# Filling an attention and feed-forward pipeline on one core: activation table loaded in advance, VectorE splits the first batch, the second batch's projections moved, dummy products on TensorE

## The chip, the cores and the metric

The kernel runs on one core of a Trainium2 chip. The metric is the device time of one execution in microseconds (us), lower is better. The engines are TensorE (PE in the profile; PEld is its weight load), VectorE (DVE), ScalarE (ACT), GpSimd (POOL) and SyncE (SP), whose queue issues all of the kernel's DMAs.

## What is computed

32 batches of 256 tokens by 128 channels. Each is layer-normalised; the normalised batch goes through 16-head attention (head size 8) and through a gated feed-forward part with token shift; both are added to the input.

```python
xn = _layernorm(x, axis=-1)
x = x + attn(xn, wq, bq, wk, bk, wv, bv, wo, bo) + ffn(xn, W_r, W_k, W_v, mu_r, mu_k)

# attn
q, k, v = (einsum('bsd,hde->bhse', x, w) + b for each of the three)
scores = softmax(einsum('bhse,bhte->bhst', q, k) * scale, axis=-1)
att = einsum('bhst,bhte->bhse', scores, v)
return att.transpose(0, 2, 1, 3).reshape(b, s, h * e) @ wo.T + bo

# ffn
xr, xk = mu * x + (1 - mu) * x_prev          # mu_r and mu_k
return sigmoid(xr @ W_r.T) * (square(relu(xk @ W_k.T)) @ W_v.T)
```

## The kernel before

The work is a software pipeline written out by hand, one step for each batch. `steps` calls each engine's `step(t, ...)` for t from -4 to 32; t = 4 to 27 stand in a hardware loop, the rest is straight code. In step t the engines work on several batches at once: t + 4 (statistics of the layer norm), t + 3 (normalise, transpose, project to q and k), t + 2 (split q and k into parts), t + 1 (row maxima of the scores), t (exponentials and their product with the values), t - 1 (output projection, store). `live(d)` says whether batch t + d exists, so the steps before t = 0 hold only the stages that already have a batch. `n(d)` is the count that a semaphore has reached when batch t + d is done.

A batch goes through these stages, by the names in the code:

- VectorE: `bn_stats`, `bn_aggr`, `var_eps`; GpSimd: `rstd` (a power), then `xn` (L316, two instructions).
- TensorE transposes `xn` (L616), ScalarE copies the result to `xn_t` (L412).
- TensorE projects `xn_t` to q in bank `misc_c` (L658) and k in `misc_b` (L662). ScalarE rounds each to bfloat16, `qk_h` (L380); VectorE subtracts, `qk_rest` (L454); GpSimd rounds the rest, `qk_m` (L328), and subtracts again, `qk_l` (L330). Three bfloat16 parts of q and k thus stand for float32.
- SyncE writes the parts to a DRAM tensor `spill` (L236 for h and m, L229 for l) and reads them back in the layout of the score products, `ops`, in two halves of two DMAs each (L214). The read waits for all five writes of the batch.
- For each of the 16 heads u, TensorE makes the scores a first time (L572, `bank_max`, two products), from 48 rows of `ops` in one half of the array's rows; VectorE reduces them to a maximum (L473). One step later it makes them a second time with the negated maxima as three added rows (L567, `bank_exp`), and ScalarE takes the exponential (L398). `LEAD` = 2: the maxima run two heads ahead, so the maxima of heads 0 and 1 of the next batch fall in u = 14 and 15 of a step. From t = 0 on, each exponential's product stands beside a maximum's product of the other half of the rows. In t = -1 the maxima of the first batch stand alone.
- In step t = -1 the first exponentials don't exist yet; TensorE ends it at u = 15 with the projections of batch 2 and the hidden product of batch 0 (L668), and t = 0 begins.

Other lines that matter: all of ScalarE's work waits for the weights' three DMAs (L368), and so does all of GpSimd's step work (L284). ScalarE's table load is put by the build ahead of its first activation. In t = -3, u = 11, VectorE fills constants (`fill_constants`, L441 to L448), ahead of the first `qk_rest`.

Of the kernel before, what the change touches and what calls it, by code (L numbers as in the profile page):

```python
# [7 lines left out]
ALU = mybir.AluOpType  # L8
# [40 lines left out]


# [5 lines left out]
def split_attention_ffn_kernel(nc, x, weights, columns, bo, out):  # L56
# [4 lines left out]
    with ExitStack() as ctx:  # L61
# [6 lines left out]
        def sem(name):  # L68
            return ctx.enter_context(nc.semaphore(name))
# [12 lines left out]
        rstd = sb("rstd", [P, ST])  # L82
        xn = sb("xn", [P, ST, D])
# [46 lines left out]
                                                         sem("rstd_done"))  # L130
        xn_done, xn_t_psum, xn_t_done = sem("xn_done"), sem("xn_t_psum"), sem("xn_t_done")
# [146 lines left out]
        def _(pool):  # L278
# [5 lines left out]
            pool.wait_ge(weights_in, 16 * N_WEIGHT_DMAS)  # L284
# [19 lines left out]
            def step(t, c, n, moved, paired, quad, live):  # L304
                p = c % 2
                if live(3):
                    pool.wait_ge(rstd_done, n(3))
                    after(pool, xn_t_psum, n(2))
                if live(2):
                    after(pool, rest_done, n(-2))  # L310
                    nc.gpsimd.tensor_tensor(x_bo[(c + 2) % TURN][:, :, :], x_in[(c + 2) % TURN][:, :, :],  # L311
                                            bo_all[:, :].unsqueeze(1).broadcast_to([P, ST, D]),
                                            ALU.add).then_inc(x_bo_done, 1)
                if live(3):
                    for i in range(ST):
                        last = nc.gpsimd.tensor_scalar(xn[:, i, :], x_in[(c + 3) % TURN][:, i, :], moments[:, i, 0:1],  # L316
                                                       rstd[:, i:i + 1], ALU.subtract, ALU.mult)
                    last.then_inc(xn_done, 1)
# [8 lines left out]
                if live(2):  # L327
                    nc.gpsimd.tensor_copy(qk_m[:, :, :], qk_rest[:, :, :]).then_inc(m_done, 1)  # L328
                    pool.wait_ge(m_done, n(2))
                    nc.gpsimd.tensor_tensor(qk_l[:, :, :], qk_rest[:, :, :], qk_m[:, :, :],  # L330
                                            ALU.subtract).then_inc(l_done, 1)
# [35 lines left out]
        def _(act):  # L367
            act.wait_ge(weights_in, 16 * N_WEIGHT_DMAS)  # L368
# [62 lines left out]
        def _(dve):  # L431
# [25 lines left out]

            by_head = misc_b[:, :].rearrange("p (k w) -> p k w", w=VW)

            def step(t, c, n, moved, paired, quad, live):  # L460
                p = c % 2
                for u in range(H):
# [12 lines left out]
                    if u == 1 and live(2):  # L475
                        take_high(1, misc_b, n(2), n(1))
                    if u == 5 and live(-1):
                        dve.wait_ge(tokens_psum, n(-1))
                        nc.vector.reciprocal(inv_den[:, :], by_head[:, :, E]).then_inc(inv_done, 1)
                        dve.wait_ge(inv_done, n(-1))  # L480
                        after(dve, att_t_psum, n(-2))
                        nc.vector.tensor_tensor(att[:, :, :], by_head[:, :, 0:E],
                                                inv_den[:, :].unsqueeze(2).broadcast_to([P, ST * H, E]),
                                                ALU.mult).then_inc(att_done, 1)
# [12 lines left out]
                    if u == 11 and live(4):  # L497
                        for i in range(ST):
# [5 lines left out]
                                                ALU.add).then_inc(var_done, 1)  # L504
                    if u == 11 and live(3) and not live(2):
                        dve.wait_ge(weights_in, 16 * N_WEIGHT_DMAS)
                        dve.wait_ge(ident_made, 1)
                        fill_constants()
# [13 lines left out]
        def _(pe):  # L522
            pe.wait_ge(ident_made, 1)

# [22 lines left out]

            def step(t, c, n, moved, paired, quad, live):
                p = c % 2
                for u in range(H):  # L550
# [3 lines left out]
                    if live(0):  # L554

                        if u % HALF == 0:
                            pe.wait_ge(shift_in[hf], moved(0, 2))
                        after(pe, exp_done[(u - 2) % H], n(0) if u >= 2 else n(-1))
                    if live(ahead):
# [4 lines left out]
                    for i in range(ST):  # L564
                        if live(0):
                            rows = slice(RG * r, RG * r + KE)
                            exp_mm = nc.tensor.matmul(bank_exp[r][:, i, :], ops[p][rows, hf, 1, pr, i * P:(i + 1) * P],  # L567
                                                      ops[p][rows, hf, 0, pr, :], start=True, stop=True)
                        if live(ahead):
# [81 lines left out]
                    if u == 15 and live(3):  # L651
                        moving = xn_t[(c + 3) % TURN][:, 1:1 + S]
                        pe.wait_ge(xn_t_done, n(3))
                        after(pe, shift_done[0], n(1))
                        after(pe, qk_rest_done[0], n(2))
                        if not live(2):
                            pe.wait_ge(weights_in, 16 * N_WEIGHT_DMAS)
                        nc.tensor.matmul(misc_c[:, 0:S], w[:, W_Q, :], moving, start=True,  # L658
                                         stop=True).then_inc(qk_psum[0], 1)
                        after(pe, val_done, n(1))  # L660
                        after(pe, qk_rest_done[1], n(2))
                        nc.tensor.matmul(misc_b[:, 0:S], w[:, W_K, :], moving, start=True,  # L662
                                         stop=True).then_inc(qk_psum[1], 1)
# [43 lines left out]
```

## Time and profile before

| | |
|---|---|
| median of 3 runs | 494.83 us (493.98 to 497.01) |
| the profiled execution's own time | 495.58 us |
| its span | 493.8 us |
| busy: PE, DVE, ACT, POOL | 457.5, 420.4, 385.2, 341.7 us |
| chain that ended last, share of PE | 85% |

The span is what the profiler sees between the first and the last instruction. The filling reaches to the first exponential product, at 39.75 us; the rest is 32 steps and the end of the pipeline. Busy TensorE time is modelled from pipelined products, so a share of 93% does not mean that the array is at its peak.

### The profile page before, as it was taken

The numbers are of one execution on the slowest core, as the hardware profiler recorded it, in microseconds if no ns is written. First come the engines' busy times: TensorE is split into PE (matmuls) and PEld (weight loads), VectorE is DVE, ScalarE is ACT, GpSimd is POOL, SyncE is SP. The second block draws the span as 40 slices with busy tenths as digits, with TensorE's granted clock in tenths as the row PEclk, the third lists the DMA queues.
The fourth block names the chain that finished last, engine by engine and source line by source line (L and its number), as shares of the span: only waits on it lengthen the run. The fifth ranks groups of instructions, "written<-read, shape, count | busy, mean of one in ns | idle before, by whom it ended". The sixth has DMA issues, their size and how long they took to land.

```text
span 493.8 us, 15503 instructions
## 1 busy us (share of the span) xinstructions
PE 457.5 (93%) x5184; PEld 260.3 (53%) x5184; DVE 420.4 (85%) x882; ACT 385.2 (78%) x833; POOL 341.7 (69%) x615
## 2 busy tenths in 40 slices
PE   1379999999999999999999999999999999999994
PEld 1125555555555555555555565556555555555552
DVE  4287899999998999899998999999998999988831
ACT  1117888887888888888888888888888888888883
POOL 6657777777787777777777777777877777776220
PEclk9999999999999999999999999999999999999997
DMA  2443454354554544345544543445544444455100
GB/s 85 127 128 81 139 153 126 95 145 130 149 152 120 151 125 118 108 134 150 150 143 126 135 127 109 124 140 150 149 124 133 131 120 119 130 141 141 46 16 22
DMA packets 85837, 60.43 MB, mean 122 GB/s; under 512 B 6192, under 2 KB 73392, under 8 KB 85808
## 3 DMA queue, kind: packets, MB, share of 16 engines
q1 hardware_dynamic: 85808, 60.06, 43.0%
q8 instruction: 16, 0.26, 0.2%
q14 instruction: 13, 0.11, 0.1%
HBM read 29.89 MB, written 29.36 MB: 120 GB/s over the span
## 4 chain that ended last, share of the span: by engine, by line
PE 85%; DVE 5%; issue 4%; ACT 2%; DMA 2%; POOL 1%; DVEq 0%; ACTq 0%; SPq 0%; POOLq 0%
PE bank_exp L567 24%; PE bank_val L535 24%; PE bank_max L572 6%; PE misc_b L638 4%; PE misc_a L589 4%; PE misc_a L608 4%; PE misc_c L658 4%; DVE neg_max L473 4%; PE misc_a L646 3%; PE misc_b L599 3%; PE misc_b L662 3%; PE misc_a L668 2%; PE misc_b L621 1%; PE misc_c L616 1%; PE misc_c L543 1%
## 5 line engine op out<-in xcount | busy, mean ns | idle before, releaser
L473 DVE TENSOR_REDUCE neg_max<-bank_max 128x2 f32<-128x512 f32 x512 | 329.5, 686 | 38.5 <-PE bank_max L572 33.4
L398 ACT ACTIVATE probs<-bank_exp 128x512 f32<-128x512 f32 x512 | 278.9, 598 | 47.2 <-PE bank_exp L567 44.8
L572 PE MATMUL bank_max<-ops 48*128 48x256 bf16 x1024 | 174.6, 278 | 10.7 <-DMA ops<-spill 8.2
L567 PE MATMUL bank_exp<-ops 51*128 51x256 bf16 x1024 | 169.5, 271 | 8.7 <-DVE neg_max L473 2.7
L535 PE MATMUL bank_val<-probs,val 128*25 128x256 f32 x2048 | 138.4, 383 | 1.2 <-ACT probs L398 1.2
L567 PEld LDWEIGHTS bank_exp<-ops 51*128 51x128 bf16 x1024 | 65.7, 94 | 110.0 <-issue 89.0
L535 PEld LDWEIGHTS bank_val<-probs,val 128*25 128x25 f32 x2048 | 56.5, 103 | 41.1 <-issue 20.2
L572 PEld LDWEIGHTS bank_max<-ops 48*128 48x128 bf16 x1024 | 61.2, 94 | 17.6 <-DMA ops<-spill 8.6
L316 POOL TENSOR_SCALAR xn<-x_in,moments,rstd 128x128 f32<-128x128 f32 x64 | 50.6, 798 | 0.1
L360 POOL TENSOR_TENSOR rstd<-var_eps,minus_half 128x2 f32<-128x2 f32 x32 | 22.8, 714 | 38.6 <-DVE var_eps L503 36.0
L355 POOL TENSOR_TENSOR mixed_x<-mixed_x,xn_t 128x512 f32<-128x512 f32 x32 | 40.6, 1270 | 2.5
L326 POOL TENSOR_TENSOR act_sq<-act_r 128x256 f32<-128x256 f32 x32 | 19.6, 612 | 28.7 <-issue 19.2
L330 POOL TENSOR_TENSOR qk_l<-qk_rest,qk_m 128x512 bf16<-128x512 f32 x32 | 37.2, 1162 | 2.6
L294 POOL TENSOR_TENSOR max_parts<-neg_max,zeros 128x16 bf16<-128x16 f32 x64 | 13.9, 218 | 31.9 <-DVE neg_max L473 31.9
L351 POOL TENSOR_TENSOR mixed_x<-dx,col 128x512 f32<-128x512 f32 x32 | 33.4, 1042 | 2.5
L373 ACT COPY shift<-misc_c 24x256 bf16<-24x256 bf16 x64 | 22.7, 355 | 14.0 <-PE misc_c L543 14.0
L380 ACT ACTIVATE qk_h<-misc_c,col 128x256 bf16<-128x256 f32 x32 | 15.2, 476 | 14.8 <-PE misc_c L658 14.2
L336 POOL TENSOR_TENSOR rest<-ffn,x_bo 128x256 f32<-128x256 f32 x32 | 23.1, 722 | 4.5 <-DVE ffn L494 4.5
L311 POOL TENSOR_TENSOR x_bo<-x_in,bo_all 128x256 f32<-128x256 f32 x32 | 23.5, 735 | 3.6 <-issue 3.4
L658 PE MATMUL misc_c<-xn_t,w 128*128 128x256 f32 x64 | 23.9, 458 | 1.8 <-ACT xn_t L412 1.8
L328 POOL CAST qk_m<-qk_rest 128x512 bf16<-128x512 f32 x32 | 19.5, 609 | 7.2 <-issue 5.1
L638 PE MATMUL misc_b<-w,xn_t 128*128 128x128 f32 x128 | 23.3, 306 | 0.0
(59 smaller groups left out, 591.7 us busy)
## 6 DMA issues: line engine op xcount, KB each, us to landing
ops<-spill SPq DMA_DIRECT2D x128, 192.0 KB, 3.4
spill<-qk_h SPq DMA_DIRECT2D x64, 192.0 KB, 3.3
spill<-qk_m SPq DMA_DIRECT2D x64, 128.0 KB, 1.9
x_in<-x SPq DMA_DIRECT2D x32, 128.0 KB, 2.1
spill<-qk_l SPq DMA_DIRECT2D x32, 128.0 KB, 1.8
y_out<-y SPq DMA_DIRECT2D x32, 128.0 KB, 1.9
ops<-shift SPq DMA_DIRECT2D x128, 6.0 KB
w<-weights SPq DMA_DIRECT2D x1, 448.0 KB, 3.1
```

The source lines that it names most:

```text
L311: nc.gpsimd.tensor_tensor(x_bo[(c + 2) % TURN][:, :, :], x_in[(c + 2) % TURN][:, :, :], bo_all[:, :].unsqueeze(1).broadcast_to([P, ST, D]) ...
L316: last = nc.gpsimd.tensor_scalar(xn[:, i, :], x_in[(c + 3) % TURN][:, i, :], moments[:, i, 0:1], rstd[:, i:i + 1], ALU.subtract, ALU.mult)
L330: nc.gpsimd.tensor_tensor(qk_l[:, :, :], qk_rest[:, :, :], qk_m[:, :, :], ALU.subtract).then_inc(l_done, 1)
L351: nc.gpsimd.tensor_tensor(mix[:, :, :], dx[:, :].unsqueeze(1).broadcast_to([P, 2, S]), col[:, C_MUR:C_MUK + 1].unsqueeze(2).broadcast_to([ ...
L355: nc.gpsimd.tensor_tensor(mix[:, :, :], mix[:, :, :], prev.unsqueeze(1).broadcast_to([P, 2, S]), ALU.add).then_inc(mix_tokens_done, 1)
L398: nc.scalar.activation(probs[g % 2][:, u % G, :, :], bank_exp[u % 2][:, :, :], ACT.Exp, scale=SCALE).then_inc(exp_done[u], 1)
L473: nc.vector.tensor_reduce(out=neg_max[hf][:, :, r, pr], in_=bank_max[v % 2][:, :, :], axis=AX_X, op=ALU.max, negate=True).then_inc(max_don ...
L535: last = nc.tensor.matmul(bank_val[SW * j:SW * j + MW, g // 2, :], weights[:, 0:MW] if fresh else weights[:, VW:VW + MW], probs[g % 2][:, ...
L567: exp_mm = nc.tensor.matmul(bank_exp[r][:, i, :], ops[p][rows, hf, 1, pr, i * P:(i + 1) * P], ops[p][rows, hf, 0, pr, :], start=True, stop ...
L572: max_mm = nc.tensor.matmul(bank_max[r][:, i, :], of[rows, max_hf, 0, max_pr, i * P:(i + 1) * P], of[rows, max_hf, 1, max_pr, :], start=Tr ...
L638: last = nc.tensor.matmul(misc_b[:, i * D:(i + 1) * D], xn_t[(c + 1) % TURN][:, 1 + i * P:1 + (i + 1) * P], w[:, W_V, :], start=True, stop ...
L658: nc.tensor.matmul(misc_c[:, 0:S], w[:, W_Q, :], moving, start=True, stop=True).then_inc(qk_psum[0], 1)
```

## The change

Six edits, all in the steps before t = 0:

- ScalarE waits for the constants alone and does one tiny `Exp` into `scratch` before it waits for the weights.
- GpSimd no longer waits for the weights before its first `rstd`; it waits for them ahead of its first `x_bo`, in t = -2.
- The first batch's `xn` is made by VectorE, `normalise_first`, right behind the first `var_eps`.
- The first batch's `qk_m` and `qk_l` are made by VectorE, `split_first`, right behind its second `qk_rest`.
- The q and k projections, now a function `project`, stand for batch 1 at u = 8 of t = -2, ahead of the first maxima; before, they stood at u = 15, behind the first two heads' maxima. All other batches keep u = 15.
- TensorE does nine 128x128 float32 products of the identity with itself (`WARM`) into `misc_a` before anything else, and, in each head whose maximum has no exponential beside it (16 heads of t = -1, two of t = -2), a dummy product into `bank_exp` beside each of the two products of the maximum, from the other half of the rows.

```diff
+WARM = 9
@@ gpsimd
-            pool.wait_ge(weights_in, 16 * N_WEIGHT_DMAS)
             pool.wait_ge(consts_made, 1)
...
-                if live(3):
+                if live(3) and live(2):
                     pool.wait_ge(rstd_done, n(3))
                     after(pool, xn_t_psum, n(2))
                 if live(2):
+                    if not live(1):
+                        pool.wait_ge(weights_in, 16 * N_WEIGHT_DMAS)
...
-                if live(3):
+                if live(3) and live(2):
                     for i in range(ST):
                         last = nc.gpsimd.tensor_scalar(xn[:, i, :], x_in[(c + 3) % TURN][:, i, :], moments[:, i, 0:1],
...
-                if live(2):
+                if live(2) and live(1):
                     nc.gpsimd.tensor_copy(qk_m[:, :, :], qk_rest[:, :, :]).then_inc(m_done, 1)
@@ scalar
+            act.wait_ge(consts_made, 1)
+            nc.scalar.activation(scratch[:, :], minus_half[:, :], ACT.Exp).then_inc(tables_in, 1)
             act.wait_ge(weights_in, 16 * N_WEIGHT_DMAS)
@@ vector
+            def normalise_first():
+                dve.wait_ge(rstd_done, 1)
+                for i in range(ST):
+                    last = nc.vector.tensor_scalar(xn[:, i, :], x_in[0][:, i, :], moments[:, i, 0:1],
+                                                   rstd[:, i:i + 1], ALU.subtract, ALU.mult)
+                last.then_inc(xn_done, 1)
+
+            def split_first():
+                dve.wait_ge(qk_rest_done[0], 1)
+                dve.wait_ge(qk_rest_done[1], 1)
+                nc.vector.tensor_copy(qk_m[:, :, :], qk_rest[:, :, :]).then_inc(m_done, 1)
+                dve.wait_ge(m_done, 1)
+                nc.vector.tensor_tensor(qk_l[:, :, :], qk_rest[:, :, :], qk_m[:, :, :], ALU.subtract).then_inc(l_done, 1)
...
                     if u == 1 and live(2):
                         take_high(1, misc_b, n(2), n(1))
+                        if not live(1):
+                            split_first()
...
                         nc.vector.tensor_scalar(var_eps[:, :], moments[:, :, 1], EPS, None,
                                                 ALU.add).then_inc(var_done, 1)
+                        if not live(3):
+                            normalise_first()
@@ tensor
             pe.wait_ge(ident_made, 1)
+            for _ in range(WARM):
+                nc.tensor.matmul(misc_a[:, 0:P], ident[:, :], ident[:, :], start=True, stop=True)
...
+            def project(c, n, live):
+                moving = xn_t[(c + 3) % TURN][:, 1:1 + S]
+                pe.wait_ge(xn_t_done, n(3))
+                after(pe, shift_done[0], n(1))
+                after(pe, qk_rest_done[0], n(2))
+                if not live(2):
+                    pe.wait_ge(weights_in, 16 * N_WEIGHT_DMAS)
+                nc.tensor.matmul(misc_c[:, 0:S], w[:, W_Q, :], moving, start=True,
+                                 stop=True).then_inc(qk_psum[0], 1)
+                after(pe, val_done, n(1))
+                after(pe, qk_rest_done[1], n(2))
+                nc.tensor.matmul(misc_b[:, 0:S], w[:, W_K, :], moving, start=True,
+                                 stop=True).then_inc(qk_psum[1], 1)
...
+                    if u == HALF and live(2) and not live(1):
+                        project(c, n, live)
...
+                        if live(ahead) and not live(0):
+
+                            rows, of = slice(RG * r, RG * r + KS), ops[(p + ahead) % 2]
+                            nc.tensor.matmul(bank_exp[r][:, i, :], of[rows, max_hf, 0, max_pr, i * P:(i + 1) * P],
+                                             of[rows, max_hf, 1, max_pr, :], start=True, stop=True)
...
-                    if u == 15 and live(3):
-                        moving = xn_t[(c + 3) % TURN][:, 1:1 + S]
...
+                    if u == 15 and live(3) and (live(1) or not live(2)):
+                        project(c, n, live)
```

Two places in the order of the instructions carry the prediction. The first is TensorE from the transposes of batch 1 (`misc_c<-ident,xn`) to the maxima of batch 0 (`bank_max`). Before:

```order
4 L616 MATMUL misc_c<-ident,xn 128x128 x2
5 L572 MATMUL bank_max<-ops 128x256 x4
6 L658 MATMUL misc_c<-xn_t,w 128x256
7 L662 MATMUL misc_b<-xn_t,w 128x256
8 L572 MATMUL bank_max<-ops 128x256 x16
```

and of the changed kernel, with the same names (`bank_exp` are the dummy products):

```order
5 L667 MATMUL misc_c<-ident,xn 128x128 x2
6 L585 MATMUL misc_c<-xn_t,w 128x256
7 L589 MATMUL misc_b<-xn_t,w 128x256
8 L618 MATMUL bank_exp<-ops 128x256
9 L623 MATMUL bank_max<-ops 128x256
10 L618 MATMUL bank_exp<-ops 128x256
11 L623 MATMUL bank_max<-ops 128x256
```

The projections of batch 1 have moved ahead of the first two heads' maxima, and each product of a maximum has a dummy ahead of it.

The second place is VectorE between the constants (`val`) and the first maxima (`neg_max`). Before:

```order
22 L454 SCALAR_TENSOR_TENSOR qk_rest<-misc_c,col,qk_h 128x256
23 L454 SCALAR_TENSOR_TENSOR qk_rest<-misc_b,col,qk_h 128x256
24 L488 BN_STATS stats<-x_in 128x6 x2
25 L499 BN_AGGR moments<-stats 128x2 x2
26 L503 TENSOR_SCALAR var_eps<-moments 128x2
27 L473 TENSOR_REDUCE neg_max<-bank_max 128x2 x2
28 L454 SCALAR_TENSOR_TENSOR qk_rest<-misc_c,col,qk_h 128x256
```

and of the changed kernel:

```order
23 L462 SCALAR_TENSOR_TENSOR qk_rest<-misc_c,col,qk_h 128x256
24 L462 SCALAR_TENSOR_TENSOR qk_rest<-misc_b,col,qk_h 128x256
25 L477 CAST qk_m<-qk_rest 128x512
26 L479 TENSOR_TENSOR qk_l<-qk_rest,qk_m 128x512
27 L513 BN_STATS stats<-x_in 128x6 x2
28 L524 BN_AGGR moments<-stats 128x2 x2
29 L528 TENSOR_SCALAR var_eps<-moments 128x2
30 L496 TENSOR_REDUCE neg_max<-bank_max 128x2 x2
31 L462 SCALAR_TENSOR_TENSOR qk_rest<-misc_c,col,qk_h 128x256
```

The two splitting instructions of batch 0 have come to VectorE; the `qk_rest` of batch 1 stay behind the first maxima.

## Rows read from the trace of the kernel before

**Rows 1.** The page: the chain that ended last, share of the span by engine.

```profile
PE 85%; DVE 5%; issue 4%; ACT 2%; DMA 2%; POOL 1%; DVEq 0%; ACTq 0%; SPq 0%; POOLq 0%
```

**Rows 2.** Timeline of the first batch: start, length, engine, line, output<-input, [idle before <-releaser].

```profile
1.18 0.29 POOL L281 TENSOR_SCALAR_AFFINE_SELECT ident<-ident 128x128 f32<-128x128 f32 x1 [0.25 <-POOL ident L279]
...
4.44 0.17 DVE L503 TENSOR_SCALAR var_eps<-moments 128x2 f32<-128x2 f32 x1
5.75 0.72 POOL L360 TENSOR_TENSOR rstd<-var_eps,minus_half 128x2 f32<-128x2 f32 x1 [2.52 <-DMA bo_all<-bo]
6.15 0.49 DVE L488 BATCH_NORM_STATS2 stats<-x_in 128x6 f32<-128x128 f32 x2 [1.53 <-DMA x_in<-x]
6.57 1.58 POOL L316 TENSOR_SCALAR xn<-x_in,moments,rstd 128x128 f32<-128x128 f32 x2
...
8.30 0.66 PE L616 MATMUL misc_c<-ident,xn 128*128 128x128 f32 x2 [8.30 <-POOL xn L316]
...
8.63 0.23 DVE L441 TENSOR_SCALAR w<-w 128x128 f32<-128x128 f32 x1
...
9.04 1.28 ACT L412 ACT_TABLE_LOAD   x1 [9.04 <-PE misc_c L616]
...
10.34 0.37 ACT L412 COPY xn_t<-misc_c 128x256 f32<-128x256 f32 x1
...
10.59 0.09 DVE L448 MEMSET val<- 128x32 f32 x1
...
10.77 1.22 PE L658 MATMUL misc_c<-xn_t,w 128*128 128x256 f32 x2 [1.81 <-ACT xn_t L412]
...
12.02 0.47 ACT L380 ACTIVATE qk_h<-misc_c,col 128x256 bf16<-128x256 f32 x1 [1.31 <-PE misc_c L658]
```

**Rows 3.** The same timeline, from the second rest to the first maximum.

```profile
13.38 0.48 DVE L454 SCALAR_TENSOR_TENSOR qk_rest<-misc_b,col,qk_h 128x256 f32<-128x256 f32 x1 [0.37 <-ACT qk_h L380]
...
14.64 0.87 SPq L236 DMA_DIRECT2D spill<-qk_m  x2
14.70 1.15 POOL L330 TENSOR_TENSOR qk_l<-qk_rest,qk_m 128x512 bf16<-128x512 f32 x1
...
15.88 0.36 SPq L229 DMA_DIRECT2D spill<-qk_l  x1
...
17.76 1.75 SPq L214 DMA_DIRECT2D ops<-spill  x4
...
22.01 0.61 PE L572 MATMUL bank_max<-ops 48*128 48x256 bf16 x4 [8.19 <-DMA ops<-spill]
```

**Rows 4.** Timeline of step t = -1, the lone maxima.

```profile
22.55 1.22 PE L658 MATMUL misc_c<-xn_t,w 128*128 128x256 f32 x2
...
24.32 0.48 DVE L454 SCALAR_TENSOR_TENSOR qk_rest<-misc_c,col,qk_h 128x256 f32<-128x256 f32 x1 [0.37 <-ACT qk_h L380]
...
25.20 1.29 DVE L473 TENSOR_REDUCE neg_max<-bank_max 128x2 f32<-128x512 f32 x2 [0.40 <-PE bank_max L572]
...
30.75 0.80 SPq L214 DMA_DIRECT2D ops<-spill  x2
...
35.01 1.29 DVE L473 TENSOR_REDUCE neg_max<-bank_max 128x2 f32<-128x512 f32 x2 [0.54 <-PE bank_max L572]
...
36.89 1.22 PE L658 MATMUL misc_c<-xn_t,w 128*128 128x256 f32 x2
...
39.75 0.28 PE L567 MATMUL bank_exp<-ops 51*128 51x256 bf16 x1
```

**Rows 5.** Windows: stretch and length, then busy us of PE, PEld, DVE, ACT, POOL, PEclk, DMA share, GB/s.

```profile
22.00:36.90 14.90, 12.40 (x49) 4.46 (x49) 12.35 (x24) 2.06 (x5) 6.67 (x12) 1.00 0.37 108
```

**Rows 6.** Timeline, the projections and the next exponential in step t = 0.

```profile
52.53 0.70 PE L658 MATMUL misc_c<-xn_t,w 128*128 128x256 f32 x2
...
54.03 0.28 PE L567 MATMUL bank_exp<-ops 51*128 51x256 bf16 x1
```

More of the change, by code:

```diff
@@ L82, in split_attention_ffn_kernel @@
         rstd = sb("rstd", [P, ST])
+        scratch = sb("scratch", [P, ST])
         xn = sb("xn", [P, ST, D])
@@ L130, in split_attention_ffn_kernel @@
                                                          sem("rstd_done"))
+        tables_in = sem("tables_in")
         xn_done, xn_t_psum, xn_t_done = sem("xn_done"), sem("xn_t_psum"), sem("xn_t_done")
@@ L650, in step @@
                         mix_values(2, n(0), n(-1), p)
-                    if u == 15 and live(3):
-                        moving = xn_t[(c + 3) % TURN][:, 1:1 + S]
[L653 to L663, printed above, removed]
+                    if u == 15 and live(3) and (live(1) or not live(2)):
+                        project(c, n, live)
                     if u == 15 and live(1):
```

## Prediction

> **What bounds the kernel now.** I read the page's chain of waits first: 85% of it is TensorE [rows 1], nearly all of that in the 32 steps, whose instructions the change leaves in the order they had. So only what comes before the first exponential product, at 39.75 us [rows 4], can move; whatever it gains should be carried through to the end, since from there every engine's order is the same. The timeline of the filling then shows three stretches.
>
> First, the chain of batch 0 up to its operands. Each link waits for the one before: `var_eps` is ready at 4.61, but GpSimd's `rstd` starts at 5.75 since it waits for the last weight DMA; `xn` takes 1.58; the transposes start at 8.30; ScalarE then loads its table for 1.28 before the copy at 10.34; the projections start at 10.77, and ScalarE takes q at 12.02 [rows 2]. VectorE ends the second rest at 13.86, GpSimd the last part at 15.85, the last write is issued at 15.88, the reads at 17.76, and TensorE's first maximum stands at 22.01 after 8.19 idle [rows 3]. Second, the lone maxima, 22.01 to 36.89, where VectorE's reductions set the pace: it is busy 12.35 of 14.9 us [rows 5], and its few gaps are 0.37 and 0.40 around batch 1's projections and 0.54 before the reduction at 35.01 [rows 4]. Third, the projections of batch 2 and the hidden product, from 36.89 to 39.75 [rows 4]: TensorE alone.
>
> One thing in the third stretch is easily missed. The windows give a granted clock of 1.00 for the whole filling [rows 5], yet the same float32 projection takes 1.22 us at 10.77, 22.55 and 36.89 and 0.70 at 52.53 [rows 2, 4, 6]. The durations say that TensorE runs the whole filling at the lower of its two levels (1.2 GHz) and from about t = 0 on at the higher (2.4 GHz). I go by the durations.
>
> **Batch 0 up to its operands.** `rstd` can start behind `var_eps`: 4.61 plus 0.1 to hand over, so 4.7 to 5.4. `xn` on VectorE: two instructions of 128x128, like the scaling at 0.23 [rows 2], some 0.5, so done at 6.0 instead of 8.15 (the bound above is GpSimd's own 1.58: 7.1). The nine dummies run from the identity (1.47) on; three products of 256 columns fill the 2.86 us from 36.89 to 39.75 [rows 4], so one of 128 costs at most 0.48, nine 4.3, and they end by 5.8: hidden behind the wait for `xn`, unless `xn` comes before 5.8. The transposes start at 6.1. From them to the first projection it was 2.47 us, of which the table load's 1.28 goes [rows 2]: 7.3. The copy came 0.02 behind the table load, so 1.28 is all that can be saved there.
>
> The Trainium skill (ScalarE: Activation LUTs, "What ACT_TABLE_LOAD costs") charges a set switch with a drain besides the load, some 2.66 us in all; this case's row shows no drain ahead of the copy, and by the page the sum would be 1.4 us better.
>
> From the projection to ScalarE's q 1.25, from there to the end of the second rest 1.84 (12.02 to 13.86): 10.4. VectorE must be free for it. Its constants took 2.05 from 8.63 to 10.68 [rows 2]; now they start about half a microsecond behind the second batch's statistics, which end at 6.64 as the input's DMA allows, and are over at about 9.2, just as the first rest is wanted. Where these constants cost nothing, the cover is thus thin, 0 to 0.2.
>
> The split moves from GpSimd (13.86 to 15.85, 1.99) to VectorE. No row shows VectorE on 512 columns from SBUF. Two instructions lie between 0.5 (the 128-column row doubled) and 2.0 (GpSimd's own); I take the reduction of 512 columns, 0.65 each, with a handover 1.4: done at 11.8. The m writes are issued at 11.1 to 12.0 (0.87 for both [rows 3]), so the l write goes out at 12.0 rather than 11.8. From there the row's own intervals: 1.88 to the reads, 4.25 to the first maximum. That is 18.1 against 22.01: **3.9 gained**; between 3.0 (`xn` and split at their upper bounds) and 4.6 (at their lower).
>
> What could eat at it: batch 1's h writes, once issued behind the first maxima, now follow the four reads directly, as q and k of batch 1 are already there. They are behind the reads in the same queue, so I charge nothing, 0.4 at most (inside the bound). GpSimd's own queue loses `xn` and the split of batch 0 and so has batch 1's `xn` earlier; its new wait for the weights at t = -2 is over by 5.7 and stops nobody.
>
> **The lone maxima.** With batch 1's projections gone from between heads 1 and 2, the gaps of 0.37 and 0.40 close: **0.8 gained** (0.3 to 1.0). The 0.54 at 35.01 is TensorE's value projection and stays at the lower level. The dummies share the array with the maxima from the other half of its rows, as exponentials do from t = 0 on, and TensorE has slack here (a pair of heads takes it 0.61, VectorE 1.29), so I charge them nothing; if they ran one after the other instead, each head would cost TensorE 0.85 against VectorE's 0.65, 18 times 0.2 = 3.6 us. Next in line is the read of batch 1's operands. It was issued at 30.75, 8.7 after the first maximum; its split ends 0.7 earlier relative to the first maximum now, and a read takes up to 4.25 [rows 3]: 12.3 after the first maximum. Head 0 of batch 1 could first be worked on once head 14 is reduced, at 35.66, or 13.65 after, now 12.9. It fits, with 0.6 to spare.
>
> **The clock.** If the dummies bring TensorE to its upper level while the maxima run, the stretch from 36.89 to 39.75 (2.86) shrinks to what it takes at 52.53 to 54.03, 1.50 [rows 4, 6]: 1.36, and part of the 0.54, say 0.15. **1.5 gained**, 0 if the level stays. For it: what stood right ahead of the change in level was three float32 products in a row, 36.89 to 39.75 [rows 4], so denser work does release it. Against it: TensorE reads 12.40 of 14.90 us busy [rows 5] and stayed low all that time, and the dummies lie beside that work, not in its gaps; they add rows of the array in use, not busy time. Nothing in the trace tells which of the two counts. The nine early dummies earn little: behind them TensorE is idle most of the time until 18, as before.
>
> The Trainium skill (TensorE: Matmul & The Clock Gate, "What's actually happening") has the lower level as the default and activity as what releases it. Read by the time that any product runs, it leaves the clock low here, since the dummies lie under the maxima; read by the work in the array, it lets it rise. The first reading is the first rival below, the second my forecast.
>
> **Sum.** 3.9 + 0.8 + 1.5 = 6.2. On the profiled execution's own 495.58 that gives 489.4; that execution is 0.75 over the median of 494.83, so for the median 488.6.
>
> **Rivals.**
>
> - *The clock stays low through the maxima* (chance 0.35). The sum is then 4.7: 490.1. If the rise then comes up to 1.8 us into the first step, that costs up to 1.5 more (at the 12.1 us for a whole step of 14.3, worked out in the last rival): to 491.6.
> - *VectorE and GpSimd get in each other's way* (0.07). During the split and the first `xn` GpSimd works on batch 1 and on the token mix, in instructions of up to 1.15 us like `qk_l` [rows 3]. If VectorE's last split instruction must wait for one, 1.15 of the 6.2 is lost: 489.8. No VectorE row of the kernel before reads two SBUF tensors, so the trace bears on it neither way. It is the Trainium skill's rule (GPSIMD Engine Reference, "Specifications"): the two engines share SBUF interfaces and contend where a VectorE instruction has two SBUF inputs, as `qk_l` has.
> - *The gain is given back or the dummies serialise* (0.04): 3.6 of 4.7 lost in the maxima as worked out above, 493.7.
> - *Slower* (0.04): the rise of the clock comes late. Before, it came just as t = 0 began. The change ends the maxima at another point, and a break in TensorE's work ahead of the dense stretch could leave the first step at the lower level. That step takes 14.3 us (39.75 to 54.03 [rows 4, 6]), 85% of it TensorE's [rows 1]; at half speed it grows by 12.1. From 40% of the step on, 5.7 us, the loss is over the 4.7 gained; a whole step gives 494.83 + 12.1 - 4.7 = 502.2. TensorE without a pause speaks against it.
>
> **How the numbers follow.** My forecast has 0.50. The low end takes the better bounds of the terms, 4.6 + 1.0 + 1.9 = 7.5, to 487.2; the high end the clock's rival with its late rise, 491.6. One per cent, about what a measurement of this kernel can tell from no change, lies at 489.9. The forecast falls below it 9 times in 10 (0.45), the low clock a third of the time (0.12), contention half (0.04): 0.61 for faster. Slower by over 1%: 0.04. The same: 0.35.
>
> **What would show it.** In the profile after: `rstd` at 4.7, `xn` on VectorE by 6.0, the copy at about 6.9, the l write at about 12.0, the first maximum near 18.1; no gap of VectorE before the second and third pair of maxima; batch 2's q projection at 0.70 rather than 1.22, the first exponential near 33.5, or near 35.0 with the low clock; the rest of the span, 454.0, unchanged. Wrong would be a first maximum behind 19, a VectorE gap ahead of batch 1's first maximum that ends on the operands' DMA, or steps of another length.

## The result, and the profile after

The changed kernel takes 488.33 us in the median of 6 runs (487.18 to 490.35), the kernel before 495.24 in 6 (493.98 to 497.01). The ratio is 0.9867, with a 95% interval of 0.9846 to 0.9889. In a second comparison, on another chip, it was 489.02 against 495.42, ratio 0.9876 (0.9857 to 0.9895). The profiled execution took 489.46, its span is 487.1 against 493.8: 6.7 less. The predicted 488.6 fits, but one of its three terms is not there, and others made up for it: that the number fits so closely is in part luck. Two of the ten executions of the kernel with two fillers a head, below, were slow ones (503.87 and 507.44) and are left out of its ratio.

The timeline of the changed kernel up to the first maximum, for comparison with [rows 2, 3]:

```profile
0.74 1.28 ACT L375 ACT_TABLE_LOAD   x1 [0.74 <-PEq L740]
...
1.53 3.84 PE L553 MATMUL misc_a<-ident 128*128 128x128 f32 x18 [1.53 <-POOL ident L285]
...
4.76 0.72 POOL L365 TENSOR_TENSOR rstd<-var_eps,minus_half 128x2 f32<-128x2 f32 x1 [1.53 <-DVE var_eps L528]
5.52 0.60 DVE L470 TENSOR_SCALAR xn<-x_in,moments,rstd 128x128 f32<-128x128 f32 x2 [0.92 <-POOL rstd L365]
...
6.18 0.44 PE L667 MATMUL misc_c<-ident,xn 128*128 128x128 f32 x2 [0.80 <-DVE xn L470]
...
6.71 0.37 ACT L420 COPY xn_t<-misc_c 128x256 f32<-128x256 f32 x1 [4.48 <-PE misc_c L667]
...
7.14 0.70 PE L585 MATMUL misc_c<-xn_t,w 128*128 128x256 f32 x2 [0.52 <-ACT xn_t L420]
...
7.88 0.47 ACT L388 ACTIVATE qk_h<-misc_c,col 128x256 bf16<-128x256 f32 x1 [0.79 <-PE misc_c L585]
...
8.87 0.45 DVE L462 SCALAR_TENSOR_TENSOR qk_rest<-misc_c,col,qk_h 128x256 f32<-128x256 f32 x1
...
9.23 0.47 DVE L462 SCALAR_TENSOR_TENSOR qk_rest<-misc_b,col,qk_h 128x256 f32<-128x256 f32 x1
9.81 0.43 DVE L477 CAST qk_m<-qk_rest 128x512 bf16<-128x512 f32 x1
...
10.27 0.69 DVE L479 TENSOR_TENSOR qk_l<-qk_rest,qk_m 128x512 bf16<-128x512 f32 x1
...
11.18 0.49 SPq L233 DMA_DIRECT2D spill<-qk_l  x1
...
13.17 1.75 SPq L218 DMA_DIRECT2D ops<-spill  x4
...
17.47 0.39 PE L618 MATMUL bank_exp<-ops 48*128 48x256 bf16 x1 [4.36 <-DMA ops<-spill]
```

The reader sees the table load gone from the chain, `rstd` behind `var_eps` instead of behind the weights, `xn` and the split on VectorE, and the first maximum at 17.48 instead of 22.01. The first projection takes 0.70, not 1.22: TensorE was at its upper level here. The first rest, at 8.87, has no gap ahead of it: VectorE comes straight from its constants.

The windows of the same kernel (stretch and length; busy us of PE, PEld, DVE, ACT, POOL; PEclk; DMA share; GB/s), for [rows 5]:

```profile
5.00:12.00 7.00, 3.04 (x14) 1.86 (x13) 6.13 (x26) 1.66 (x4) 5.24 (x7) 0.98 0.43 128
12.00:17.40 5.40, 1.11 (x3) 0.34 (x1) 0.58 (x1) 0.84 (x2) 4.78 (x6) 0.50 0.65 182
17.40:31.40 14.00, 12.02 (x80) 4.22 (x80) 12.09 (x24) 1.11 (x3) 6.65 (x12) 0.50 0.36 105
31.40:34.30 2.90, 2.90 (x10) 1.86 (x8) 1.41 (x3) 0.95 (x2) 2.73 (x6) 0.50 0.32 94
35.80:48.00 12.20, 11.44 (x128) 6.23 (x130) 10.87 (x23) 10.16 (x23) 8.58 (x17) 1.00 0.28 84
```

PEclk is the answer to the term that failed: 0.98 behind the early products, then 0.50 from 12 us to 34.3, through all the maxima with their dummies. The way from the second stretch into t = 0, for [rows 4]:

```profile
31.03 1.29 DVE L496 TENSOR_REDUCE neg_max<-bank_max 128x2 f32<-128x512 f32 x2 [0.20 <-PE bank_max L623]
```

```profile
31.43 1.22 PE L585 MATMUL misc_c<-xn_t,w 128*128 128x256 f32 x2
32.45 1.06 PE L589 MATMUL misc_b<-xn_t,w 128*128 128x256 f32 x2
33.30 1.06 PE L708 MATMUL misc_a<-mixed_x,w 128*128 128x256 f32 x2
34.29 0.39 PE L613 MATMUL bank_exp<-ops 51*128 51x256 bf16 x1
```

Batch 2's projection still takes 1.22 and the first exponential comes 2.86 behind it, exactly as before. Where the 6.7 us of the two profiled executions went:

| stretch | before | after | gained | forecast |
|---|---|---|---|---|
| to the first maximum | 22.01 | 17.48 | 4.5 | 3.9 |
| first maximum to batch 2's projection | 14.88 | 13.95 | 0.9 | 0.8 |
| projection to first exponential | 2.86 | 2.86 | 0 | 1.5, with part of a gap before it |
| step t = 0, to the next first exponential | 14.28 | 13.60 | 0.7 | 0 |
| next first exponential to the last `y` but one | 427.5 | 427.5 | 0 | 0 |
| last `y` behind the one before | 9.47 | 8.96 | 0.5 | 0 |

The last three lines follow from 39.75, 54.03, 481.56 and 491.03 before and 34.29, 47.89, 475.40 and 484.36 after, the starts of exponential products and of `y`. From the first exponential to the end of the span it is 452.8, where the forecast had 454.0, unchanged.

### The profile page after: what moved, and what is told of

The parts are those of the page before. It is cut to its first block, busy times and chain, and to the rows that moved or that the text cites. A ratio compares the mean times of both kernels' runs of the same rounds, so it can differ in the third digit from the quotient of the medians.

```text
span 487.1 us, 15612 instructions
## 1 busy us (share of the span) xinstructions
PE 461.3 (95%) x5238; PEld 263.7 (54%) x5238; DVE 422.2 (87%) x886; ACT 385.6 (79%) x834; POOL 339.6 (70%) x611
## 4 chain that ended last, share of the span: by engine, by line
PE 86%; DVE 6%; issue 4%; ACT 2%; DMA 1%; DVEq 0%; ACTq 0%; SPq 0%; POOL 0%; POOLq 0%
PE bank_exp L613 24%; PE bank_val L565 24%; PE bank_max L623 5%; PE misc_b L689 4%; PE misc_a L640 4%; PE misc_a L659 4%; DVE neg_max L496 4%; PE misc_c L585 3%; PE misc_a L697 3%; PE misc_b L650 3%; PE misc_a L708 2%; PE misc_b L589 2%; PE misc_c L573 1%; PE misc_c L667 1%; PE misc_b L672 1%
## 5 line engine op out<-in xcount | busy, mean ns | idle before, releaser
L623 PE MATMUL bank_max<-ops 48*128 48x256 bf16 x1024 | 176.8, 279 | 0.0
L321 POOL TENSOR_SCALAR xn<-x_in,moments,rstd 128x128 f32<-128x128 f32 x62 | 49.3, 801 | 0.0
L335 POOL TENSOR_TENSOR qk_l<-qk_rest,qk_m 128x512 bf16<-128x512 f32 x31 | 36.1, 1164 | 2.5
L381 ACT COPY shift<-misc_c 24x256 bf16<-24x256 bf16 x64 | 22.7, 355 | 14.2 <-PE misc_c L573 14.2
L420 ACT COPY xn_t<-misc_c 128x256 f32<-128x256 f32 x32 | 12.0, 374 | 21.7 <-PE misc_c L667 17.9
L640 PE MATMUL misc_a<-w,mixed_x 128*128 128x128 f32 x128 | 22.8, 300 | 0.0
```

The source lines that it names most:

```text
L623: max_mm = nc.tensor.matmul(bank_max[r][:, i, :], of[rows, max_hf, 0, max_pr, i * P:(i + 1) * P], of[rows, max_hf, 1, max_pr, :], start=Tr ...
L640: last = nc.tensor.matmul(misc_a[:, i * D:(i + 1) * D], mixed_x[p][:, 0, i * P:(i + 1) * P], w[:, W_R, :], start=True, stop=True)
```

## The experiments

In all of them the time to the first maximum, the first exponential and PEclk are read from the timeline and the windows; "before" in a ratio was run on the same chip.

**Without the dummies beside the maxima**

```diff
-                        if live(ahead) and not live(0):
-
-                            rows, of = slice(RG * r, RG * r + KS), ops[(p + ahead) % 2]
-                            nc.tensor.matmul(bank_exp[r][:, i, :], of[rows, max_hf, 0, max_pr, i * P:(i + 1) * P],
-                                             of[rows, max_hf, 1, max_pr, :], start=True, stop=True)
```

> The changed kernel without the dummy products beside the lone maxima. Theory A (they do nothing, since the granted clock in the changed kernel's own trace is 0.50 from 12 to 34.3 us with them): the first exponential product stays at 34.3 within 0.3, the time at 488.3 within 1. Theory B (they earn the forecast 1.5 us in most executions and the profiled one was an exception): the time rises to about 489.8.

First maximum at 17.32, first exponential at 34.10, PEclk 0.50 in between, projection 1.22, span 487.1: the same profile as with them. Its median was 490.01 (0.9915, 0.9883 to 0.9947), 1.7 above the changed kernel's, which theory A did not allow for. So both were run again, on one chip:

> The changed kernel once more, in one call with the kernel without the dummies beside the maxima. Theory A (those dummies do nothing): both kernels' ratios to the kernel before overlap, the first exponential products stand within 0.3 us of each other. Theory B (they help in most executions, by the clock): this kernel is 1 to 1.7 us ahead.

> The changed kernel without the dummies beside the maxima, once more and on the same chip as the changed kernel. Theory A: the same time as the changed kernel, the clock at 0.50 through the maxima in both. Theory B: 1 to 1.7 us later, and a clock that rises ahead of the first exponential in the changed kernel alone.

489.02 with the dummies (0.9876, 0.9857 to 0.9895) and 489.62 without (0.9885, 0.9864 to 0.9906); first exponentials at 34.02 and 33.99. The windows of the maxima, with the dummies and then without:

```profile
17.40:31.40 14.00, 12.08 (x81) 4.31 (x78) 12.35 (x25) 1.11 (x3) 6.83 (x13) 0.50 0.39 116
```

```profile
17.40:31.40 14.00, 11.14 (x45) 3.54 (x42) 12.42 (x25) 1.11 (x3) 6.87 (x13) 0.50 0.40 119
```

TensorE has 36 products more and only 0.9 us more busy time; the clock reads 0.50 in both. From the first maximum to the first exponential it is 16.81 in both traces with the dummies, 16.78 and 16.77 in both without. Theory A holds: these 36 products neither help nor hurt.

**Without the nine early products**

```diff
-            for _ in range(WARM):
-                nc.tensor.matmul(misc_a[:, 0:P], ident[:, :], ident[:, :], start=True, stop=True)
```

> The changed kernel without the nine early products. Theory A (they buy the higher level for the first transposes and projections, at 6.2 to 8.3 us): the first transposes take 0.66 instead of 0.44, the first projection 1.22 instead of 0.70, and the first maximum comes 0.3 to 0.8 later than 17.5; the time is about 488.9. Theory B (VectorE's constants cover it): the first maximum stays within 0.2 of 17.5.

Transposes 0.66, first projection 1.22, first maximum at 17.91: 0.4 later than in the first profile of the changed kernel and 0.7 later than in the second (17.21). The l write goes out 1.0 later, at 12.14; part of that is `qk_l` on VectorE, 0.98 here and 0.69 there. 490.67, ratio 0.9900 (0.9866 to 0.9934), where 488.9 was expected. Theory A, for the start. In this execution the level rose only at 40.3, 5.6 us into t = 0.

**Dense products ahead of the maxima, with and without the dummies beside**

```diff
                     if u == HALF and live(2) and not live(1):
                         project(c, n, live)
+                        for _ in range(14):
+                            nc.tensor.matmul(misc_a[:, 0:P], ident[:, :], ident[:, :], start=True, stop=True)
```

> The changed kernel with 14 more 128x128 float32 products of the identity behind the projections of batch 1, in the wait for the operands (13.1 to 17.4 us). Theory A (dense work raises the clock, and the dummies beside the maxima then hold it): granted clock 1.00 when the maxima begin and until the end, batch 2's q projection at 0.70, the first exponential about 1.4 to 2 us earlier, at 32.3 to 32.9, the time about 486.7. Theory B (nothing beside reduction-paced maxima holds the clock): it falls back during the maxima, the first exponential stays at about 34.

> The same 14 dense products, without the dummies beside the maxima. If the dummies beside hold the clock that the dense ones raise: here it falls back to 0.50 during the maxima and the first exponential stands at about 34, the time at 488. If they do nothing either way: this trace has the same clock and the same first exponential as the run with both.

The windows with the dummies beside:

```profile
12.50:16.80 4.30, 4.30 (x19) 4.03 (x19) 0.12 (x1) 0.95 (x2) 4.14 (x6) 0.50 0.55 154
16.80:23.60 6.80, 4.41 (x46) 2.36 (x45) 4.87 (x9) 0.00 (x0) 1.56 (x3) 1.00 0.33 86
23.60:34.60 11.00, 10.21 (x56) 4.82 (x54) 8.52 (x18) 2.05 (x5) 7.89 (x16) 0.50 0.40 122
```

and without:

```profile
12.50:14.90 2.40, 2.40 (x10) 2.13 (x10) 0.37 (x1) 0.84 (x2) 2.28 (x3) 0.50 0.24 76
14.90:21.70 6.80, 4.51 (x35) 2.93 (x33) 3.81 (x8) 0.00 (x0) 2.71 (x4) 1.00 0.60 167
21.70:34.00 12.30, 10.86 (x38) 4.61 (x38) 9.69 (x20) 2.06 (x5) 8.94 (x17) 0.50 0.36 111
```

Dense float32 work raises the level in both, and it falls back among the maxima in both, 5.3 us behind the first one with the dummies and 4.3 without. The dummies beside them do not hold it: theory B. First exponentials at 34.69 and 34.02; 490.19 (0.9903, 0.9871 to 0.9935) and 490.69 (0.9918, 0.9895 to 0.9942). In the first, the level rose so late that the 14 products ended at 18.36 and the maxima started right behind them, at 18.30, though the reads were issued at 13.21 as usual.

**Filling TensorE's gaps instead**

```diff
                     if live(ahead):
                         max_mm.then_inc(max_scores[v], 1)
+                    if live(ahead) and not live(0) and u < H - 1:
+                        for _ in range(1):
+                            nc.tensor.matmul(misc_a[:, 0:P], ident[:, :], ident[:, :], start=True, stop=True)
```

The second kernel has `range(2)`. Both have no dummies beside the maxima, and 8 dense products ahead of them.

> The changed kernel without the dummies beside the maxima, with 8 dense float32 products in the wait for the operands and one 128x128 float32 product of the identity behind each lone maximum's products, so in TensorE's gaps and not beside its work. Theory A (busy time counts, so filling the gaps raises and holds the level): granted clock 1.00 in most of 18 to 33 us, batch 2's q projection at 0.70, the first exponential near 32.8, and no late rise behind it; the time about 486.5. Theory B (rows of the array in use count and one product is too little): the clock falls back as in the runs with the dense products alone, and at the lower level the fillers cost up to 0.2 us a head.

> The same with two filler products a head. At the upper level they take 0.43 of the 0.65 us that a head takes VectorE, so they should be free and hold the clock; at the lower level they take 0.85 and slow each head until the clock rises. Theory A: granted clock 1.00 from the first maxima on, the first exponential near 32.8. Theory B: it falls or rises late, the first exponential comes 1 to 3 us later than 34.3.

One filler a head: the level rises at 14.2, falls at 21.0, and then each head takes 1.26 instead of 0.65 us, 0.6 more where up to 0.2 was expected, as VectorE's timeline shows:

```profile
25.16 0.69 DVE L496 TENSOR_REDUCE neg_max<-bank_max 128x2 f32<-128x512 f32 x1 [0.57 <-PE bank_max L620]
26.43 0.69 DVE L496 TENSOR_REDUCE neg_max<-bank_max 128x2 f32<-128x512 f32 x1 [0.57 <-PE bank_max L620]
```

First exponential at 41.85, 497.50, ratio 1.0041 (1.0014 to 1.0067). The windows of this run:

```profile
18.00:21.00 3.00, 2.77 (x16) 1.40 (x16) 2.57 (x5) 0.00 (x0) 0.00 (x0) 1.00 0.61 177
21.00:41.50 20.50, 20.50 (x67) 11.28 (x66) 11.59 (x22) 1.72 (x5) 9.37 (x17) 0.50 0.22 66
```

From 21.0 to 41.5 the profile has TensorE busy in all of the 20.50 us, and the granted clock reads 0.50 throughout. So theory A, that busy time counts, does not come out of this run, although its gaps were filled. Two fillers a head:

```profile
15.00:17.40 2.40, 1.06 (x10) 0.87 (x9) 0.00 (x0) 0.00 (x0) 2.08 (x3) 0.99 0.93 268
17.40:34.20 16.80, 16.80 (x108) 11.04 (x108) 12.89 (x24) 1.11 (x3) 7.00 (x14) 1.00 0.35 107
34.20:35.70 1.50, 1.50 (x8) 1.05 (x6) 0.91 (x2) 0.72 (x2) 1.50 (x3) 1.00 0.07 11
```

Here the level stays up from 15.0 on, with TensorE busy in all of the 16.8 us, and projections and hidden product take the forecast 1.50 (34.24 to 35.74). But the fillers stand in order ahead of the next head; with a head's two products of the maximum they take TensorE 0.96, more than VectorE's 0.65, and so each head takes 0.96:

```profile
23.84 0.69 DVE L496 TENSOR_REDUCE neg_max<-bank_max 128x2 f32<-128x512 f32 x1 [0.27 <-PE bank_max L620]
24.80 0.69 DVE L496 TENSOR_REDUCE neg_max<-bank_max 128x2 f32<-128x512 f32 x1 [0.27 <-PE bank_max L620]
```

The first exponential comes at 35.74, later than the changed kernel's 34.29; 491.61 (0.9923, 0.9898 to 0.9947). The price for the clock is more than the 1.4 that it gives. Why two fillers hold the level, while one neither holds it nor brings it back with TensorE busy throughout, no run tells.

**Batch 1's projections back behind the first maxima**

```diff
-                    if u == HALF and live(2) and not live(1):
-                        project(c, n, live)
-                    if u == 15 and live(3) and (live(1) or not live(2)):
+                    if u == 15 and live(3):
```

> The changed kernel with batch 1's projections back at u = 15 of t = -2, behind the first two heads' maxima. By the prediction's second term the gaps of 0.37 and 0.40 us come back: the first maximum stays near 17.5, the way from it to the first exponential grows from 16.8 to about 17.6, the time to about 489.1. Rival: the gap closed for another reason (the rests of batch 1 are late anyway), and nothing moves.

First maximum at 17.25, first exponential at 35.45: 18.2 between them, against 16.8, so 1.4 more where 0.8 was expected. VectorE's timeline has the gaps back:

```profile
19.98 0.48 DVE L462 SCALAR_TENSOR_TENSOR qk_rest<-misc_c,col,qk_h 128x256 f32<-128x256 f32 x1 [0.79 <-ACT qk_h L388]
20.87 1.29 DVE L496 TENSOR_REDUCE neg_max<-bank_max 128x2 f32<-128x512 f32 x2 [0.41 <-PE bank_max L621]
```

0.79 and 0.41 rather than 0.37 and 0.40: with a dummy ahead of each of the first four maxima's products the projections start 0.96 behind the first maximum, without them it was 0.54 [rows 3, 4]. So the move is worth 1.4 in this order of instructions and 0.9 against the kernel before, which has no dummies. 489.94, ratio 0.9890 (0.9847 to 0.9933): the time alone would not have told it.

**The first split back on GpSimd**

```diff
                         take_high(1, misc_b, n(2), n(1))
-                        if not live(1):
-                            split_first()
...
-                if live(2) and live(1):
+                if live(2):
                     nc.gpsimd.tensor_copy(qk_m[:, :, :], qk_rest[:, :, :]).then_inc(m_done, 1)
```

> The changed kernel with the first batch's qk_m and qk_l back on GpSimd. In the changed kernel VectorE takes 0.43 + 0.69 us for them, GpSimd took 0.61 + 1.15. Theory A: only the difference shows, the l write goes out 0.7 to 0.9 later, the first maximum at about 18.3. Theory B (GpSimd's queue matters): in the changed order GpSimd is at batch 1's xn (1.75 us from 8.63 to 10.38) when the rests are ready at 9.7, so the split also waits for it: the first maximum at about 18.9, the time at 489.7.

The l write goes out at 12.10 instead of 11.18, the first maximum comes at 18.18, 0.7 to 1.0 later: theory A's number, but not by its reason alone. GpSimd was at batch 1's `xn` when the rests were ready at 9.77, and took up the split at 10.22: its queue costs 0.45, not the 0.7 of theory B. The split itself then takes it 1.86, against 1.26 from the second rest to the end of the split on VectorE. 489.57, ratio 0.9892 (0.9846 to 0.9937).

**The table load back, and `xn` back on GpSimd** (one execution each, for the profile)

```diff
-            act.wait_ge(consts_made, 1)
-            nc.scalar.activation(scratch[:, :], minus_half[:, :], ACT.Exp).then_inc(tables_in, 1)
```

> The changed kernel without the early Exp, so with the table load back in front of the first copy. By the prediction's chain the copy comes 1.28 later (6.71 to 8.0), and so does everything up to the first maximum, less what VectorE's constants covered: they end at 8.98 and the first rest now starts at 8.87, so the whole 1.28 less about 0.6 of waiting for them shows: first maximum at 18.2 to 18.8. Rival: a switch costs 2.66 with its drain, and the first maximum comes at 19.5 or later.

```diff
-                if live(3) and live(2):
+                if live(3):
...
-                        if not live(3):
-                            normalise_first()
```

> The changed kernel with the first batch's xn back on GpSimd, which still starts its rstd without waiting for the weights. xn takes 1.58 instead of 0.60, so the transposes start about 1.0 later, at 7.2; VectorE's constants start later as well, since its aggregate waits for xn. First maximum 0.9 to 1.1 later than 17.5, at 18.4 to 18.6.

They took 490.53 and 490.73. With the table load back, the first maximum is at 19.41, later than expected. The timeline:

```profile
6.18 0.69 PE L665 MATMUL misc_c<-ident,xn 128*128 128x128 f32 x2 [0.44 <-DVE xn L468]
...
6.96 1.28 ACT L418 ACT_TABLE_LOAD   x1 [6.96 <-PE misc_c L665]
...
8.25 0.37 ACT L418 COPY xn_t<-misc_c 128x256 f32<-128x256 f32 x1
...
8.68 1.22 PE L583 MATMUL misc_c<-xn_t,w 128*128 128x256 f32 x2 [1.81 <-ACT xn_t L418]
...
12.35 0.98 DVE L477 TENSOR_TENSOR qk_l<-qk_rest,qk_m 128x512 bf16<-128x512 f32 x1
```

It is not the rival's drain: the copy starts right behind the 1.28 of the load. In this execution the nine early products did not raise the level, so transposes and projections took 0.69 and 1.22 and added 0.25 + 0.52; and the last split instruction took 0.98 instead of 0.69. With `xn` on GpSimd the first maximum was at 19.00, in an execution with the same two extras: `xn` 1.58 instead of 0.60 is 1.0 of the 1.5 to 1.8.

## Why the prediction was right or wrong

**Batch 0 up to its operands, 3.9: right in mechanism, 0.6 to 0.9 too small.** The chain went as worked out, link by link: `rstd` at 4.76 (4.7), transposes at 6.18 (6.1), no drain behind the table load. What was sized too long were the products behind it: I let transposes and projections run at the lower level, and they ran at the upper one, 0.22 and 0.52 shorter. That is the work of the nine early products, of which the prediction said that they "earn little"; without them the first maximum came 0.4 to 0.7 later. The split took 1.26 from the end of the second rest (9.70 to 10.96) and not 1.4, some 0.7 less than GpSimd's. The thin cover over VectorE's constants did not hold once the projections came early: ScalarE had q ready at 8.35, and the first rest, which followed 0.04 behind that in the kernel before (12.49, 12.53), followed 0.52 behind, at 8.87, when the constants were done. They cost some 0.4 there, the next thing to move; no run has tried it.

**The lone maxima, 0.8: right, measured 0.9** in the pair of profiles; undone in the changed kernel it was 1.4. Batch 1's operands were in time, as worked out. The dummies beside cost nothing, also as charged.

**The clock, 1.5: wrong, 0 measured.** This was the step on which the forecast differed from its first rival, and the rival was right: "the clock stays low through the maxima". The prediction asked whether rows of the array in use or busy time count. The runs say that products in the other half of the rows, under the maxima, change nothing, twice from the lower level (PEclk 0.50 with and without) and once from the upper (it falls with and without). Two fillers a head in the gaps hold it. But neither is busy time the answer: with one filler TensorE was busy for 20.50 of 20.50 us at 0.50. What does count stays open. The price of 1.4 for that stretch was right: it took 1.50 where the level was held.

**What stood in its place.** The rival's sum, 4.7, would have given 490.1. The measured gain is 6.4 to 6.9 in the medians. 5.5 of it is ahead of the first exponential, by 4.5 + 0.9 (5.7 in the second profile of the changed kernel). The rest is 0.7 in step t = 0 and 0.5 at the end, in the profiled pair.

In step t = 0 of the kernel before, the reads went out at 48.03, 3.55 behind the start of the l write and 8.28 behind the first exponential; TensorE then idled 0.82 ahead of the next batch's first maxima. SyncE's rows of before, then of after:

```profile
44.48 1.22 SPq L229 DMA_DIRECT2D spill<-qk_l  x1
48.03 0.80 SPq L214 DMA_DIRECT2D ops<-spill  x2
```

```profile
39.23 0.36 SPq L233 DMA_DIRECT2D spill<-qk_l  x1
41.03 0.80 SPq L218 DMA_DIRECT2D ops<-spill  x2
```

It is 1.80 and 6.74 now. Such a late read is not the kernel before's alone: the kernel with two fillers a head had it too, 3.92 behind a write issued in 0.36 (40.46, 44.38), with TensorE idle for 1.00 and a step of 14.45; and in later steps every trace has reads that are more than 3 us behind their l write. The long issue alone does not do it: 1.05 in one execution of the kernel without the dummies beside (38.92) left the reads at 41.51, 2.59 behind.

The 0.5 at the end is the clock again. TensorE's level falls ahead of the last `y`, at 486.9 before and 482.7 after, which is 5.4 and 7.3 behind the last `y` but one. So the last batch's transposes ran mostly at the lower level before and at the upper one after:

```profile
486.69 0.93 PE L599 MATMUL misc_b<-ident,mixed 128*128 128x128 f32 x4 [0.71 <-ACT mixed L404]
488.52 0.69 PE L621 MATMUL misc_b<-ident,att 128*128 128x128 f32 x2 [0.91 <-DVE att L482]
```

```profile
480.53 0.66 PE L650 MATMUL misc_b<-ident,mixed 128*128 128x128 f32 x4 [0.71 <-ACT mixed L412]
482.10 0.44 PE L672 MATMUL misc_b<-ident,att 128*128 128x128 f32 x2 [0.91 <-DVE att L507]
```

The traces of the experiments go the same way: where the level fell 3.2 behind the last `y` but one, the last stretch took 10.5; where it fell 9.4 behind, 8.5. Whether late reads and an early fall are more frequent in the kernel before can't be said from its one trace, so some 0.7 to 1.4 of the medians' gain is not shown to come from the change. This part, and the first term's 0.6 to 0.9, stood in for the missing 1.5; that they came to about as much is luck.

**Contention of VectorE and GpSimd: real, and smaller.** The instruction that the rival named, `qk_l`, took 0.29 longer in four of the traces, not 1.15, and nothing longer in the profiled execution of the changed kernel. It is taken up below.

**The slower rival** had a late rise of the clock. Late rises did occur, 5.6 to 6.0 us behind the first exponential (in the kernels without the early products, with 14 dense ones, and once without the dummies beside). From the first exponential to the first `y` these executions took 26.6 to 26.8 against 25.4 with a rise 0.8 to 1.7 behind: 1.1 to 1.3 lost. I had priced each us of a step at the lower level at 0.85, taking TensorE's 85% of the chain as wholly proportional to its clock; the 4 to 5 us more that these executions spent there cost about a third of that. The loss scatters the times, and does not decide between the kernels. A small slip of the sum: the low end, 494.83 less 7.5, is 487.3 and not 487.2.

## What to carry to other kernels

A filling is a chain that runs once: take its waits one by one, and give each link to the engine that is idle and quickest, as here `xn` and the split to VectorE. Dummy products that lay under other products did nothing for the clock here. In TensorE's gaps two of them a head held it and one did not, though TensorE was then busy throughout, so measure the clock rather than count busy time. In order behind a semaphore they cost the work behind them more than the clock gave back; they paid where TensorE waited for something long and the chain's own products came next, at the start. A link made faster uncovers the next one, as here VectorE's constants. When a prediction hits, compare its terms with the stretches of both traces before believing its reasons.

## What the runs showed of the hardware that was not expected

VectorE and GpSimd hold each other up. A `var_eps` of 128x2, 0.17 us elsewhere, took 0.90 in the changed kernel and ended at 12.58, with GpSimd's `mixed_x`, which ended at 12.55:

```profile
11.51 1.04 POOL L356 TENSOR_TENSOR mixed_x<-dx,col 128x512 f32<-128x512 f32 x1
11.68 0.90 DVE L528 TENSOR_SCALAR var_eps<-moments 128x2 f32<-128x2 f32 x1
```

It ended 0.02 to 0.03 behind `mixed_x` in all twelve traces in which VectorE splits the first batch. In the same way `qk_l` on VectorE took 0.98 where GpSimd's `dx` was running when it started (four traces) and 0.69 where it started first (eight), and then it was `dx` that took 1.08 where GpSimd alone does it in 0.61. The Trainium skill (GPSIMD Engine Reference, "Specifications") names two SBUF inputs and the two-port mode as the cases of contention; the rows agree for `qk_l` with 0.3 us, a quarter of the price that the prediction put on it. `var_eps` has one tensor input; that it ends with a GpSimd instruction is seen in these rows, its cause is not shown.

The moments at which TensorE's level changes move from execution to execution: the rise behind the nine early products came between 4.6 and 6.6 us, and in three of the twelve traces that have these products not at all; the rise around t = 0 came between 0.8 and 6.0 us behind the first exponential in the changed kernel and its variants without fillers.

The windows gave a granted clock of 1.00 for the whole filling of the kernel before [rows 5], where the durations said half. In the trace of after, which holds a change of level early on, the windows and the durations agree from there on. A granted clock ahead of the first recorded change is thus not to be trusted.
